# A 16-head cross-attention stage: preparation on tiles of 32 columns, paired mask products, joined capping, first keys inside the norm

## The reference, cut to what matters

```
def _L2_xattn_ref(query, key, value, mask, W_q, W_k, W_v, W_o):
    D_MODEL = 128; NUM_HEADS = 16; D_K = 8
    Q = _split(query @ W_q.T)
    K = _split(key @ W_k.T)
    V = _split(value @ W_v.T)
    scores = jnp.einsum('bhqd,bhkd->bhqk', Q, K) / jnp.sqrt(jnp.float32(D_K))
    scores = jnp.where(mask, -jnp.inf, scores)
    attn_w = jax.nn.softmax(scores, axis=-1)
    attn_w = jnp.nan_to_num(attn_w, nan=0.0)
    out = jnp.einsum('bhqk,bhkd->bhqd', attn_w, V)
    ...
    return merged @ W_o.T

x = x + _L2_xattn_ref(_layernorm(x), ctx_1024, ctx_1024, mask, ...)
```

## Time and profile before

| | us |
|---|---|
| runs of the kernel before (3): median, lowest, highest | 2998.79, 2996.69, 2999.44 |
| profiled execution: span from its first instruction to its last (it has no other time of its own) | 2996.3 |
| TensorE busy in it | 2624.0 (88%) |
| VectorE busy | 2034.1 (68%) |
| ScalarE busy | 1390.4 (46%) |
| GpSimd busy | 431.4 (14%) |
| mean granted TensorE clock, as a share of 2.4 GHz | 0.933 |

### The profile page before, as it was taken

One profiled execution on the slowest core, in us unless ns is written; L12 is line 12 of the kernel. 1 busy time (PEld: TensorE's weight loads), 2 busy tenths in 40 slices (PEclk: granted clock), 3 DMA queues, 4 the chain that ended last, 5 costly groups with the idle time before them and its releaser, 6 DMA issues. The chain is left out here.

```text
span 2996.3 us, 66594 instructions
## 1 busy us (share of the span) xinstructions
PE 2624.0 (88%) x27038; PEld 1716.3 (57%) x27038; DVE 2034.1 (68%) x6821; ACT 1390.4 (46%) x2529; POOL 431.4 (14%) x299
## 2 busy tenths in 40 slices
PE   7998745798999899999999999999988999888634
PEld 5776543455777565566565555566645555565423
DVE  5554514576211389899999899889768876565786
ACT  3441312565333245555555555555459964434511
POOL 0000030441000000000000000000006960563200
PEclk9998876898999899999999999999998999999866
DMA  7970311000000100000000000000002210991000
GB/s 232 336 248 10 123 55 22 8 3 17 15 22 8 52 24 24 24 24 24 24 25 34 24 24 24 24 24 13 2 9 95 92 57 2 352 369 43 2 0 14
DMA packets 73344, 189.00 MB, mean 63 GB/s; under 512 B 12130, under 2 KB 39717, under 8 KB 73008
## 3 DMA queue, kind: packets, MB, share of 16 engines
q1 hardware_dynamic: 64912, 156.68, 15.8%
q10 hardware_dynamic: 7104, 26.23, 2.4%
q0 software_dynamic: 1024, 1.85, 0.2%
HBM read 154.19 MB, written 30.79 MB: 62 GB/s over the span
## 5 line engine op out<-in xcount | busy, mean ns | idle before, releaser
L3119 DVE CUSTOM_DVE_ANT_0 L_xattn_junk<-L_xattn_ps_mx,L_xattn_shift 128x512 f32<-128x512 f32 (+1 forms) x1024 | 544.8, 569 | 113.2 <-issue 103.7
L3200 ACT ACTIVATE L_xattn_pT<-L_xattn_ps_st 128x512 f32<-128x512 f32 x768 | 416.9, 594 | 403.9 <-PE L_xattn_ps_st L2958 403.9
L2971 PE MATMUL L_xattn_ps_mx<-L_xattn_kT,L_xattn_qb 32*128 32x512 f32 (+1 forms) x2048 | 480.6, 552 | 0.0
L2958 PE MATMUL L_xattn_ps_st<-L_xattn_qb,L_xattn_kT 32*128 32x256 f32 (+1 forms) x3328 | 455.0, 383 | 0.0
L3165 DVE TENSOR_TENSOR L_xattn_pT<-L_xattn_pT,L_xattn_capT 128x512 f32<-128x512 f32 (+1 forms) x710 | 423.0, 636 | 29.9 <-ACT L_xattn_pT L3200 26.9
L2958 PEld LDWEIGHTS L_xattn_ps_st<-L_xattn_qb,L_xattn_kT 32*128 32x128 f32 (+1 forms) x3328 | 299.7, 181 | 18.6
L3018 PE MATMUL L_xattn_ps_pv<-L_xattn_pT,L_xattn_v 128*17 128x128 f32 x6656 | 263.6, 276 | 0.0
L3018 PEld LDWEIGHTS L_xattn_ps_pv<-L_xattn_pT,L_xattn_v 128*17 128x17 f32 x6656 | 146.4, 97 | 163.5 <-issue 76.1
L2984 PE MATMUL L_xattn_ps_st<-L_xattn_less,L_xattn_ones_b 3*128 3x512 bf16 x768 | 178.1, 386 | 0.9 <-ACT L_xattn_pT L3200 0.8
L2925 POOL TENSOR_TENSOR L_xattn_qb<-ln_sq,L_xattn_four 128x256 f32<-128x256 f32 x32 | 19.6, 614 | 1089.5 <-PE L_xattn_ps_st L2958 1069.3
L2971 PEld LDWEIGHTS L_xattn_ps_mx<-L_xattn_kT,L_xattn_qb 32*128 32x128 f32 x2048 | 151.9, 184 | 23.9 <-DVE L_xattn_tops L3119 14.6
(11 more groups left out here) (622 smaller groups left out, 5050.5 us busy)
## 6 DMA issues: line engine op xcount, KB each, us to landing
L_xattn_ctxT<-context_turned SPq DMA_DIRECT2D x64, 800.5 KB, 6.1
context_turned<-L_xattn_ctxT SPq DMA_DIRECT2D x32, 800.5 KB, 9.4
L_xattn_ctx<-in_ctx SPq DMA_DIRECT2D x32, 768.0 KB
L_xattn_ctx<-in_ctx ACTq DMA_DIRECT2D x32, 768.0 KB
L_attn_cc<-scratch_rows SPq DMA_DIRECT2D x32, 512.0 KB, 3.6
L_xattn_out_keys<-scratch_q SPq DMA_DIRECT2D x32, 200.1 KB, 9.8
L_ffn_w<-in_L_ffn_w SPq DMA_DIRECT2D x4, 1024.0 KB, 10.3
L_ffn_w<-in_L_ffn_W SPq DMA_DIRECT2D x16, 256.0 KB, 3.1
```

What stands on the lines that cost most here:

```text
L2958: last = nc.tensor.matmul(st[0:chunk[j], w % 3, 256 * c2:256 * c2 + 256], kT[n % 3][r:r + 32, P * j:P * j + chunk[j]], qb[n % 3][r:r + 32, ...
L2971: last = nc.tensor.matmul(mx[:, w % 3, to:to + width], qb[n % 3][32 * g:32 * g + 32, 2 * (p % 2):2 * (p % 2) + 2, :].rearrange("p h q -> p ...
L3119: last = nc.vector.tensor_tensor_reduce(out=junk[:, w % 3, to:to + width], in0=mx[:, w % 3, to:to + width], in1=shift[:, k0:k0 + width], s ...
L3200: nc.scalar.activation(pT[b % HELD][:, :, gi, :], st[:, w % 3, :].rearrange("p (c k) -> p c k", c=2), ACT.Exp)\
```

## The change

1. All units of `prepare` run as products of 32 output columns at four column positions (`tile_position=(0, 32 * q)`), where one product of 128 columns stood. M, E1 were transpositions and are now products with an identity, M in bf16.
2. The units are spread anew (PREPARED), ON_TENSOR is (1, 4, 8, 11), and values wait for their own V piece, maxima for their own K piece.
3. `less_out` is called after `keys_by_query`, with both score buffers of a bundle, one in the rows 0 to 63 and one in the rows 64 to 127 of the array.
4. `less_max` of the second score buffer comes after `query_by_keys`.
5. VectorE caps a bundle's probabilities with one instruction for both buffers, one bundle later. The copies of `pv` and of yT go to ScalarE, and `negated_parts` has six instructions instead of eight.
6. The four K units of batch 0 run inside the norm, its V units at bundles -17, -15, -13 and -11; FIRST is -18. The masks are prepared after the norm, the caps on GpSimd and turned at bundle -12. Three of four query pieces are scaled by ScalarE. The transfers are issued in another order (wk, wq, context of batch 0 first).
7. `kept_busy` is gone.

The diff, cut:

```
-    FIRST, LAST = -LEAD - ROUND, ROUND * (B - 1) + ROUND + 10
-    PREPARED = {0: ("K", 0), 2: ("V", 0), 3: ("K", 1), 4: ("V", 1), 5: ("K", 2), 6: ("V", 2), 7: ("K", 3), 9: ("V", 3)}
-    ON_TENSOR = (4, 7, 9)
+    FIRST, LAST = -LEAD, ROUND * (B - 1) + ROUND + 10
+    AHEAD = -LEAD - ROUND
+    PREPARED = {0: ("K", 0), 2: ("V", 0), 4: ("K", 1), 6: ("V", 1), 9: ("K", 2), 11: ("V", 2), 13: ("K", 3), 17: ("V", 3)}
+    FIRST_VALUES = {-17: 0, -15: 1, -13: 2, -11: 3}
+    CAP_TURNED = -12
+    ON_TENSOR = (1, 4, 8, 11)
...
-            for dst, src in ((wq, "wq"), (wk, "wk"), (wv, "wv"), (wo, "wo")):
-                sp.dma_start(dst[:, :], a[f"{name}_{src}"]).then_inc(loaded, 16)
+            sp.dma_start(wk[:, :], a[f"{name}_wk"]).then_inc(ctx_in[0], 16)
+            sp.dma_start(wq[:, :], a[f"{name}_wq"]).then_inc(ctx_in[0], 16)
+            sp.dma_start(ctxT[:, 0, :], c.turned[0, :, :]).then_inc(ctx_in[0], 16)
...
+            def keys_unit(to, n, m):
+                width = SPANS[m][1]
+                for q in range(4):
+                    last = nc.tensor.matmul(to[32 * q:32 * q + 32, 0:width], wk[:, 32 * q:32 * q + 32],
+                                            ctxT[:, n % 2, 512 * m:512 * m + width], start=True, stop=True, tile_position=(0, 32 * q))
+                last.then_inc(prep_done, 1)
+            def between_turns(i):
+                if i == 1:
+                    pe.wait_ge(ctx_in[0], 48)
+                    keys_unit(first_keys[0], 0, 0)
+                    keys_unit(first_keys[1], 0, 1)
+                elif i == 2:
+                    pe.wait_ge(*A.at("ln_T0"))
+                    nc.tensor.matmul(qps[0], wq[:, :], c.xnT[:, 0:512], start=True, stop=True).then_inc(PE.did("q0"), 1)
+                    keys_unit(first_keys[2], 0, 2)
+                elif i == 3:
+                    keys_unit(first_keys[3], 0, 3)
...
+            def less_out(b, step):
+                for c2 in (0, 1):
+                    j = 2 * step + c2
+                    for gi in (0, 1):
+                        rows = slice(S * gi, S * gi + S)
+                        last = nc.tensor.matmul(st[0:chunk[j], (2 * b + gi) % 3, 256 * c2:256 * c2 + 256],
+                                                shift[rows, P * j:P * j + chunk[j]], four_turns[rows, :, :].rearrange("p h q -> p (h q)"),
+                                                start=False, stop=(c2 == 1), tile_position=(S * gi, 0))
...
                     for j in range(4 * m, 4 * m + part[m]):
                         to = P * (j - 4 * m)
-                        last = nc.tensor.matmul(prep[0:chunk[j], to:to + P], ctxT[:, n % 2, P * j:P * j + chunk[j]], wv[:, :],
-                                                start=True, stop=True)
+                        for k in range(0, chunk[j], 32):
+                            wide = min(32, chunk[j] - k)
+                            last = nc.tensor.matmul(prep[k:k + wide, to:to + P], ctxT[:, n % 2, P * j + k:P * j + k + wide], wv[:, :],
+                                                    start=True, stop=True, tile_position=(0, k))
...
                 if now:
-                    less_max(b, *now)
-                    if masked_here(b):
-                        less_out(b, *now[1:])
+                    less_max(b, *now, 0)
                 if then:
...
                     query_by_keys(b + LEAD, *then)
                 if now:
+                    less_max(b, *now, 1)
                     keys_by_query(b, *now, 0)
                     keys_by_query(b, *now, 1)
+                    if masked_here(b):
+                        less_out(b, now[1])
                 for x in values_at(b):
                     values(x)
                 prepare(early(b))
                 prepare(late(b))
-                kept_busy(b)
...
+            def cap_probabilities(b, n, step, half):
+                k, j = (P, (2 * step, 2 * step + 2)) if step < 6 else (KREST, (KC - 1, KC))
+                x = pT[b % HELD][0:k, 0:j[1] - j[0], :, :].rearrange("p c g (h q) -> p c (g h) q", q=S)
+                dve.wait_ge(exped, 2 * b + 2)
+                nc.vector.tensor_tensor(x, x, capT[0:k, j[0]:j[1], :].unsqueeze(2).broadcast_to([k, j[1] - j[0], 8, S]), ALU.min)
```

More of the change, by code:

```diff
@@ L261, in ln_tensor @@
         last.then_inc(PE.did(f"{g}_PT{i}"), 1)
+        if between:
+            between(i)
 def start(c):
@@ L2851, in early @@
         def early(b):
[L2853 to L2857, removed]
+            for n in range(1, B):
+                i = b - ROUND * n - AHEAD
+                if i in PREPARED:
+                    kind, m = PREPARED[i]
+                    return kind, n, m
+            return ("V", 0, FIRST_VALUES[b]) if b in FIRST_VALUES else None
         def late(b):
@@ L2865, in late @@
             return None
-        prep_at = {}
+        prep_at = {("K", 0, m): m + 1 for m in range(4)}
         for b in range(FIRST, LAST):
@@ L2881, in capped_by @@
         def capped_by(b):
-            return 2 * sum(not masked_here(x) for x in range(b + 1))
+            return sum(not masked_here(x) for x in range(b + 1))
         def values_at(b):
@@ L2955, in keys_by_query @@
                     return
+                ends = c2 == 1 or j == KC - 1
                 for gi in (0, 1):
@@ L3007, in values @@
                     pe.wait_ge(capped, capped_by(b))
+                if b % ROUND % 4 == 0:
+                    pe.wait_ge(prep_read, prep_at["V", n, step // 2])
                 if b % ROUND == 0:
-                    pe.wait_ge(prep_read, prep_at["V", n, 3])
                     if n:
                         pe.wait_ge(pv_copied, n)
-                    nc.tensor.matmul(pv[:, 0:256], zero_b[0:32, :], less[n % 2][0:32, 0, :], start=True, stop=False)
+                    for q in range(4):
+                        nc.tensor.matmul(pv[32 * q:32 * q + 32, 0:256], zero_b[:, :], less[n % 2][:, 0, :], start=True, stop=False,
+                                         tile_position=(0, 32 * q))
                 for c2 in (0, 1):
@@ L3042, in prepare @@
                     for e in (0, 1):
-                        last = nc.tensor.transpose(prep[:, P * e:P * e + P], parts[:, e, :, :].rearrange("p g j -> p (g j)"), c.ident[:, :])
+                        for q in range(4):
+                            last = nc.tensor.matmul(prep[32 * q:32 * q + 32, P * e:P * e + P], parts[:, e, q, :], ident_b[:, :],
+                                                    start=True, stop=True, tile_position=(0, 32 * q))
                 elif kind == "E1":
```

239 lines of the change are left out of this document (125 added, 114 removed).

## The result

| | us |
|---|---|
| kernel before, 4 runs on the same chip: median (lowest, highest) | 2998.35 (2996.69, 2999.44) |
| kernel after, 4 runs | 2908.53 (2903.92, 2912.41) |
| ratio, 95% interval | 0.9698, 0.9685 to 0.9712 |
| predicted; range | 2886; 2856 to 2922 |
| profiled execution of after: span; mean granted clock | 2902.1; 0.921 |

The change gains 90 us, 3%. The forecast was 112, so the time lies inside the range and 22 above the forecast. The profiled execution is the fastest of the four: 94.2 less than the span of before.

A forecast was written before the change was run, and what follows sets the result against it. TensorE was taken to bound the stage, with VectorE near its end. Gains of 71 (steady part), 26.6 (beginning), 9 (maxima-only bundles) and 5 (end), 112 us, off the median 2998.8 gave 2887, rounded 2886; range 2856 to 2922.

The forecast's parts named there:

- Preparation, 1.87 per round: TensorE's preparation units on 32-column tiles: 8.64 before, 6.77 us after per round, with weight loads hidden.
- The rival that they show: Weight loads of 32-column tiles not hidden: +4 us per round, total 3001, or 2960 if half shows; 8%.
- Masks, 0.32 each at the end: Mask products on TensorE: 0.32 us in four bundles per round instead of 0.76 in three, gain 1.00.
- The prediction's serial rival: Masks last in a bundle but not side by side: cost 26 us, total 2912; no chance given.
- Waits at the score buffers, 0.43 and 0.76: TensorE's second subtraction waits for an earlier exponential behind positions 1 and 3 of a round, 1.19 us in all.
- Steady part, 71: 430 bundles with maxima and scores: 30.2 rounds, each 33.1 us instead of 35.44, gain 71 us.
- Order of the second subtraction worth nothing to TensorE: Second subtraction behind the maxima: no TensorE gain, since maxima and scores both fill 1.18 us; VectorE can start earlier.
- Joined capping: One VectorE capping for both buffers: 1.23 us against 1.29 for two, 0.06 less in ten bundles per round.
- The beginning, 26.6: Stage start to first maxima: first maxima at 992.9 instead of 1019.55, gain 26.6 us, bounds 22 and 29.
- The bundles with maxima only, 9: 18 bundles from first maxima to first subtraction: 32.5 us instead of 41.7, gain 9, bounds 6 and 11.
- The end, 5: Last 18 bundles, without maxima: 1.94 us each instead of 2.33, gain 5; bounds 8, and -12 if the clock falls.
- The clock as a rival: Without fillers the granted clock falls to half through the whole stage: total over 3300 us; 4%.

The follow-up runs named there:

- 3: Changed kernel with every preparation unit (K, V, M, E1, E2, E3) as whole 128-column work again, at the new places; 2947.45 us, ratio 0.9836.
- 6: Changed kernel with mask products serial in one half of the rows, ahead of the maxima, at the same four positions; 2958.47 us, ratio 0.9867.
- 2: Changed kernel with four filler transpositions in each of the maxima-only bundles -10 to -1; 2901.71 us, ratio 0.9679.
- 7: Changed kernel with the second subtraction straight behind the first, ahead of the maxima; 2906.04 us, ratio 0.9691.
- 8: Changed kernel with the joined capping split into one instruction per score buffer, still one bundle later; 2914.83 us, ratio 0.9714.
- 9: Changed kernel with four filler transpositions in each of the six bundles 433 to 438 alone; 2892.88 us, ratio 0.9646.
- 4: Changed kernel with K2 at position 3 instead of 5 and the last V unit of batch 0 at bundle -10; 2892.87 us, ratio 0.9650.
- 10: Changed kernel with the K2 and V unit moves of 4 and the six-bundle fillers of 9; 2882.45 us, ratio 0.9611.
- 11: As 10, with the masked bundle at position 3 instead of 4; 2881.97 us, ratio 0.9607.
- 1: Changed kernel with four filler transpositions per bundle back in the bundles without maxima, behind bundle 430; 2898.72 us, ratio 0.9669.

## Why the prediction was right, and where it was off

- **Preparation, 1.87 per round:** right. Undoing it costs 1.85 (3). The loads of four 32-column tiles don't show. A load's record is even 110 ns long, where the prediction had 26 one after another; but the four of a step start about 6 ns apart and lie side by side, under the step of 0.11 before theirs. The rival that they show is out. The Trainium skill (TensorE: Matmul & The Clock Gate, Part 3, "The mechanism") lets a load overlap a product only in another row group. All four tiles here are in the same one, and the trace disagrees with that sentence for 32 columns as the earlier trace rows did for 17. The same section also allows a load ahead of running products where it goes to the background weight buffer; that would fit, but the records don't say where a load goes.
- **Masks, 0.32 each at the end:** right (1.20 to 1.52). Against serial ones at the same four places, 1.91 (6). The prediction's serial rival (0.22 more in each bundle) priced another arrangement, serial but still last, which no run tried. The starts in after, in two pairs, show that the masks do run side by side.
- **Waits at the score buffers, 0.43 and 0.76:** 0.41 and 0.98. The 0.22 more at position 4 is time that the bundle before it does not take: from its start to the next it is 0.96, not 1.18, and the two bundles together are 4.98 against 4.88 forecast. **Own values, 0.3:** 0.39. **VectorE 28.9:** 28.9. The round is 33.32 instead of 33.1.
- **Steady part, 71:** 68.2, and this is closer than the working deserves. With the true round of before it is 30.2 x (35.50 - 33.32) = 65.8. The rest is the clock. In before a fall of 10.2 us, from 2129.3 on, lies in the steady part and lost some 4.4 us (an estimate, with the 0.43 per us found below). In after 5.3 us of the first fall lie in it; number 2, with the same code there and the full clock, took 1018.4 instead of 1021.0, so they cost 2.6. That makes 67.6. The gain per round was forecast as 2.34 and is 2.18, and before's fall hid that by luck.
- **Order of the second subtraction worth nothing to TensorE:** right (7: 33.35 against 33.32). By the Trainium skill (same page, Part 2, on the weight load) products stay in program order. In after the second subtraction (1502.16) starts before the second pair of maximum passes (1502.29) of products that precede it. What is out of order, here as in the earlier trace rows, is the second pass of a float32 product; the first passes of those products start ahead of the subtraction, as written (1501.75 and 1501.80). So the trace disagrees for second passes only.
- **Joined capping:** priced by VectorE's busy time alone, at nothing for TensorE. It gives 0.13 per round through the own values (8), about 4 us.
- **The beginning, 26.6:** 28.4. The clock was back up at 980.4, before the first K units had run at half of it for long; that was the bound "clock up early", 29. The first two took 2.37 us, from 979.50 on, where the prediction had 3.8. No run takes this part of the change back by itself; it rests on the two traces. Another 1.9 lie ahead of the stage, where the change has nothing: in the twelve traces with the changed kernel's beginning the stage starts anywhere from 971.8 to 977.3, so this is the spread of single executions.
- **The bundles with maxima only, 9:** 1.2, below the bound of 6. Two things. The count of units missed K0 and V0 of the third batch, which run at the bundles -4 and -2: about 2.1. And the clock was at half from 1014.6 to 1029.8, 15.2 us. Number 9 gives the price: with the same code in this phase it had 26.7 us at half clock and took 45.5, so 5.0 more for 11.5 us more, 0.43 per us. Numbers 4, 10 and 11, with nearly the same code, had 20.2 and took 42.1, 0.32 per us. That makes 4.9 to 6.6 for 15.2. With the 2.1 it is 7.0 to 8.7, around the 7.8 that are missing, but no run had this phase wholly at the full clock, so the second term is an estimate and not shown.
- **The end, 5:** -6.7; this is the step that failed most, and what was mis-sized is the clock. The prediction set -12 as the bound in case it fell here and 5 as the value; it fell, and cost 53.5 - 39.6 = 13.9 against number 9, which has fillers in six bundles. Number 2, whose end is the code of after without any filler, was at half clock there for 4.2 us instead of 42 and took 38.9, so against it the clock cost 14.6. Numbers 3 and 6, with other units and masks, agree (39.1 and 38.7). Runs 1, 9 and 10 show it from the other side. At the full clock the mechanism was right in the main: 1.89 per bundle over 439 to 444, with E2 and E3 in two of them, where 1.94 was forecast. The same six took 2.43 before, not 2.33. The whole gain there is 7.2 (9) to 7.9 (2), close to the bound of 8.

2.8 from the steady part, 7.8 from the maxima-only bundles and 11.7 from the end, less 1.8, 1.9 and 1.2 gained elsewhere, are 17.4. Of the rest of the 22.5 between forecast and median, 4.6 is that the profiled run was the fastest of the four (2903.9 against 2908.5). Another 1.2 is a slip of the prediction: its terms give 2887.2, not 2886.

**The clock as a rival** was given 4% for a fall through the whole stage; that was out, the steady part being at 1.00. What came was a fall at both ends of it, where few or no maxima, K and V units run, 62.6 us in all. It should have stood as a case of its own, at some 20 us less gain and with far more than a few per cent: in before it fell too, for 10.2 us from 2129.3 on, 20 us ahead of that phase.

## What to carry to other kernels

A saving that takes work off a busy engine and the fillers between it has to be priced with the clock in both states, at the ends of the stage above all; fillers in six bundles (24 transpositions) kept 14 us. The five kernels with fillers in the end all stayed at the full clock there but for at most its last 1.4 us; of the seven without, four lost about 14 us in the profiled execution and three did not. Between products of 32 columns in the same division of the array no wait showed here, so bring neighbouring units to one division before anything else. And when two limits lie within half a microsecond of each other per bundle, removing the first gives little: of 1.37 here the second took 0.62 back and the moved unit 0.3, and 0.43 were left.

## What the runs showed of the hardware that I had not expected

- How long the clock stays low differs widely at the same or nearly the same code. From a fall in the end phase without fillers it stayed low for 54.6 to 58 us in after, 4, 7 and 8 (39 to 42 of them inside the phase), and for 3.4 us in 2, 3 and 6. The ends took 52.5 to 53.5 and 38.7 to 39.1. It differs between executions of one kernel too: the five of number 2 have mean clocks from 0.923 to 0.930 and times from 2893.04 to 2905.93. In the beginning it was 20.5 us in after and 30.7 in number 9, whose code is the same there. The fall in the beginning came in all eleven kernels tried and in after, between 1008.1 and 1020.0 us. What brings it stays open: in after it followed waits of 0.78 and 0.44 us for VectorE in bundles of short maxima, but in number 2 no wait stood in the 3 us ahead of it.
- At half clock a microsecond loses less than half. In the six bundles 439 to 444 it is 0.43 (3.34 against 1.89), in the maxima-only bundles 0.32 to 0.43 (numbers 4 and 9 against after), and over the whole low part of the end, with its waits, a third: 13.9 in 42.1.
- A change of division between units and values of the same 32-column kind costs nothing that can be seen: the unit starts 0.45 after the values, their four steps of 0.11. Ahead of a whole-array unit it is 0.56, so 0.11 more (3).
